# A layer with linear attention and a LoRA feed-forward: the shared expert's down factors are multiplied into the down weights on chip

## What is computed

```python
gate = x @ W_gate + lora(x, sA_gate, sB_gate) + expert_lora(x, A_gate, B_gate, w)
up = x @ W_up + lora(x, sA_up, sB_up) + expert_lora(x, A_up, B_up, w)
hidden = silu(gate) * up
out = hidden @ W_down + lora(hidden, sA_down, sB_down) + expert_lora(hidden, A_down, B_down, w)
```

## Time and profile before

| | before |
|---|---|
| median of 3 runs | 721.21 us (720.41 to 721.88) |
| the profiled execution: its own time | 720.7 us |
| the profiled execution: its span | 718.9 us |
| PE busy | 701.2 us (98%) |
| DVE busy | 376.2 us (52%) |
| ACT busy | 260.7 us (36%) |
| POOL busy | 122.3 us (17%) |
| read from HBM, written | 51.56 MB, 20.97 MB |

### The profile page before, as it was taken

One profiled execution on the slowest core, in us unless ns is written; L12 is line 12 of the kernel. 1 busy time (PEld: TensorE's weight loads), 2 busy tenths in 40 slices (PEclk: granted clock), 3 DMA queues, 4 the chain that ended last, 5 costly groups with the idle time before them and its releaser, 6 DMA issues.

```text
span 718.9 us, 10792 instructions
## 1 busy us (share of the span) xinstructions
PE 701.2 (98%) x3690; PEld 563.2 (78%) x3690; DVE 376.2 (52%) x715; ACT 260.7 (36%) x402; POOL 122.3 (17%) x293
## 2 busy tenths in 40 slices
PE   7999999989999999999999999999999999999997
PEld 5788888876776677888888888888888888888886
DVE  5666556677575675444427444336534435544434
ACT  4344334564331432333333333324333224323322
POOL 3554555420642651000000000000000000000000
PEclk9999999999999999999999999999999999999999
DMA  7756656326746635000010500001600001300001
GB/s 241 270 194 195 202 192 210 125 111 251 274 142 236 221 131 217 18 0 0 0 49 37 208 0 0 0 4 54 233 0 0 0 0 58 117 0 0 0 0 60
DMA packets 22755, 72.79 MB, mean 101 GB/s; under 512 B 2688, under 2 KB 2944, under 8 KB 20688
## 3 DMA queue, kind: packets, MB, share of 16 engines
q1 hardware_dynamic: 22560, 72.24, 28.4%
q0 software_dynamic: 176, 0.30, 0.2%
HBM read 51.56 MB, written 20.97 MB: 101 GB/s over the span
## 4 chain that ended last, share of the span: by engine, by line
PE 90%; DVE 4%; issue 2%; POOL 2%; ACT 1%; DMA 1%; SPq 0%; DVEq 0%; POOLq 0%; ACTq 0%
PE bank L1115 19%; PE bank L1116 19%; PE bank L1117 19%; PE bank L1328 17%; PE bank L1303 6%; PE bank L1315 4%; PE bank L1228 2%; DMA w_raw<-in_wkT 1%; PE bank L1180 1%; PE bank L1132 1%; PE bank L1152 1%; PE bank L1144 1%; PE bank L1236 1%; PE bank L1344 0%; PE bank L1346 0%
## 5 line engine op out<-in xcount | busy, mean ns | idle before, releaser
L1115 PE MATMUL bank<-x,up_h 128*128 (+1 forms) x352 | 137.5, 391 | 2.1 <-DVE qf L980 1.2
L1116 PE MATMUL bank<-x,up_h 128*128 (+1 forms) x352 | 137.3, 390 | 0.0
L1117 PE MATMUL bank<-x,up_l 128*128 (+1 forms) x352 | 137.0, 389 | 0.0
L1048 DVE TENSOR_TENSOR hf<-bank,silu 128x512 f32<-128x512 f32 x44 | 30.4, 692 | 162.3 <-issue 142.6
L1115 PEld LDWEIGHTS bank<-x,up_h 128*128 128x128 f32 x352 | 66.1, 188 | 18.8 <-issue 2.1
L597 ACT ACTIVATE hid_h<-hf 128x512 fp32r<-128x512 f32 x44 | 27.8, 632 | 142.9 <-DVE hf L1048 142.9
L1117 PEld LDWEIGHTS bank<-x,up_l 128*128 128x128 f32 x352 | 66.1, 188 | 14.1
L1116 PEld LDWEIGHTS bank<-x,up_h 128*128 128x128 f32 x352 | 66.1, 188 | 13.8
L793 DVE TENSOR_TENSOR up_l<-up_raw,up_h 128x1024 fp32r<-128x1024 f32 x45 | 55.6, 1235 | 31.4 <-ACT up_h L597 31.4
L1328 PE MATMUL bank<-dn_h,hid_h 128*128 128x512 f32 x176 | 69.5, 395 | 0.0
L1328 PE MATMUL bank<-dn_l,hid_h 128*128 128x512 f32 x176 | 69.1, 392 | 0.0
(11 more groups left out here) (167 smaller groups left out, 1228.3 us busy)
## 6 DMA issues: line engine op xcount, KB each, us to landing
x<-scr_x SPq DMA_DIRECT2D x8, 2048.0 KB, 7.5
up_raw<-in_ffn_up SPq DMA_DIRECT2D x11, 768.0 KB, 5.5
scr_x<-xt SPq DMA_DIRECT2D x16, 512.0 KB, 4.4
xin<-in_x SPq DMA_DIRECT2D x16, 256.0 KB, 5.8
scr_z<-zt SPq DMA_DIRECT2D x16, 256.0 KB, 2.2
x3r<-in_x SPq DMA_DIRECT2D x16, 256.0 KB, 3.5
scr_att<-x3r SPq DMA_DIRECT2D x16, 256.0 KB, 2.1
z<-scr_z SPq DMA_DIRECT2D x4, 1024.0 KB, 5.0
```

What stands on the lines that cost most here:

```text
L1048: nc.vector.tensor_tensor(hf[:], ps_u[:], silu[:], ALU.mult).then_inc(h_done, 1)
L1115: nc.tensor.matmul(dst, lh, rh, start=start, stop=False, **kw)
L1116: nc.tensor.matmul(dst, lh, rl, start=False, stop=False, **kw)
L1117: return nc.tensor.matmul(dst, ll, rh, start=False, stop=stop, **kw)
```

## The change

`W_down + sA_down @ sB_down / 8` is formed on chip and replaces W_down; the shared expert's columns leave the down operand, which shrinks from 592 to 576 columns. The product is made in stage 3: after `queries(g, (1, 2, 3))` of groups 1, 2 and 3, PE does one float32 matmul for each of 4, 4 and 3 chunks (`shared_down`), with 32 rows of contraction (8 of them not zero) at four different row positions of the array in turn, 128 output rows by 512 columns, into banks 2, 3, 4 and 5. DVE adds each bank, times 1/8, to the chunk in `dn_raw` in place, after its `queries` and ahead of its `attention(g - 1, (0, 1))`. PE's `denominators(g)`, which writes bank 2, now also waits for these additions (`dnm_done`), and ACT's first split of down weights waits for all 11. All down weights have to be there by then: SP loads them in stage 1, two chunks where it loaded one, and the two new constants (192 and 256 KB) ahead of wo and wq. PE's loop over groups 1 and 2 is unrolled.

`lora_down` takes two matmuls a chunk for three: the first has 128 stationary columns, the experts' 64 high and 64 low columns side by side, with the high part of the hidden values moving; the second has the 64 high columns with the low part moving. For that the split down weights lie in one tile `dn` of 9 blocks of 64 columns, high and low parts of a block next to each other, so the 512 columns that line 1328 reads are eight pieces of 64 with gaps of 64. Rows 64 to 127 of ps_zd then hold the low part's share; they are weighted like the others (`weights_of` copies twice, and two memsets at the start of the late stage go), zd1 takes all 128 rows, and `lora_down_lo` is one subtraction in place of two. ACT's extra rounding of 8 rows of `bdn` in stage 2 goes, and `bdn_done`, for which POOL and SP wait, comes from DVE.

```diff
@@ -46,2 +46,4 @@
-DNR = ER + 2 * R
-DNC = D + DNR
+DNC = D + ER
+DNB = DNC // ER
+SHG = P // DK
+SHN = -(-FC // SHG)
@@ -53 +55 @@
-STAGE2_LOADS = 8
+STAGE2_LOADS = 10
@@ -60 +62 @@
-    "ffn_up": (P, FC, UPC), "ffn_dn": (P, FC, DNC), "b_dn": (P, 2, D),
+    "ffn_up": (P, FC, UPC), "ffn_dn": (P, FC, DNC), "b_dn": (P, 2, D), "sa_dn": (P, SHN, P), "sb_dn": (P, D),
@@ -78,0 +81,2 @@
+        sa_dn = sb("sa_dn_sb", [P, SHN, P])
+        sb_dn = sb("sb_dn_sb", [P, D])
@@ -198,2 +202,2 @@
-        dn_h = at("dn_h", [P, 2, DNC], F32R)
-        dn_l = at("dn_l", [P, 2, DNC], F32R)
+        dn = at("dn", [P, 2, DNB, 2, ER], F32R)
+        dn_h, dn_l = dn[:, :, :, 0], dn[:, :, :, 1]
@@ -219,0 +224 @@
+        ps_sh = bank[2:6]
...
@@ -287,0 +291,2 @@
+        sh_ready = sem("sh_ready")
+        dnm_done = sem("dnm_done")
@@ -397 +402 @@
-            for dst, name in ((hmask, "headmask"), (hcol, "headcol"), (hrow_raw, "headrow"), (bdn_raw, "b_dn")):
+            for dst, name in ((hmask, "headmask"), (hcol, "headcol"), (hrow_raw, "headrow"), (bdn_raw, "b_dn"), (sa_dn, "sa_dn"), (sb_dn, "sb_dn")):
@@ -405,2 +410 @@
-            def load_ffn(c):
-
+            def load_up(c):
@@ -407,0 +412,2 @@
+
+            def load_dn(c):
@@ -414 +420,2 @@
-                load_ffn(p)
+                load_up(p)
+                load_dn(2 * p)
@@ -417 +424,4 @@
-            load_ffn(TILES // 2 - 3)
+                load_dn(2 * p + 1)
+            load_up(TILES // 2 - 3)
+            for c in range(TILES - 6, FC):
+                load_dn(c)
...
@@ -718,2 +727,0 @@
-            act.wait_ge(bdnl_done, 1)
-            round_to(bdn[SH:SH + R, 1], bdn_raw[SH:SH + R, 1]).then_inc(bdn_done, 1)
@@ -737 +745 @@
-                round_to(dn_h[:, s, :], dn_raw[:, bass.ds(c, 1), :].rearrange("p o n -> p (o n)")).then_inc(dnh_done, 1)
+                round_to(dn_h[:, s], dn_raw[:, bass.ds(c, 1), :].rearrange("p o (b n) -> p (o b) n", n=ER)).then_inc(dnh_done, 1)
@@ -761,2 +769,2 @@
-                round_to(zd1[0:ER, :], zw[0:ER, :])
-                round_to(zd2[0:DNR, :], zw[0:DNR, :]).then_inc(zdh_done, 1)
+                round_to(zd1[:], zw[:])
+                round_to(zd2[0:ER, :], zw[0:ER, :]).then_inc(zdh_done, 1)
@@ -778 +786 @@
-            act.wait_ge(dn_in, 16 * FC)
+            act.wait_ge(dnm_done, FC)
@@ -958,0 +967,8 @@
+            def shared_down(g, n=SHG):
+
+                for i in range(n):
+                    c = (g - 1) * SHG + i
+                    dve.wait_ge(sh_ready, c + 1)
+                    w = dn_raw[:, bass.ds(c, 1), 0:D].rearrange("p o n -> p (o n)")
+                    nc.vector.scalar_tensor_tensor(w, ps_sh[i][:], RSCALE, w, ALU.mult, ALU.add).then_inc(dnm_done, 1)
+
@@ -961,0 +978 @@
+                    shared_down(g, FC - (GROUPS - 2) * SHG if then is not None else SHG)
@@ -1010 +1027 @@
-            sub(bdn[0:SH2, 1], bdn_raw[0:SH2, 1], bdn[0:SH2, 1]).then_inc(bdnl_done, 1)
+            sub(bdn[0:ER, 1], bdn_raw[0:ER, 1], bdn[0:ER, 1]).then_inc(bdn_done, 1)
@@ -1033 +1050 @@
-                sub(dn_l[:, s, :], dn_raw[:, bass.ds(c, 1), :].rearrange("p o n -> p (o n)"), dn_h[:, s, :]
+                sub(dn_l[:, s], dn_raw[:, bass.ds(c, 1), :].rearrange("p o (b n) -> p (o b) n", n=ER), dn_h[:, s]
@@ -1056,3 +1073,4 @@
-                nc.vector.tensor_copy(wcur[:, :, 0:ER].rearrange("p j (e r) -> p j e r", e=E),
-                                      wtok[:, bass.ds(g * GT, GT), :].unsqueeze(3).to_broadcast([P, GT, E, R])
-                                      ).then_inc(wcur_done, 1)
+                for a in range(2):
+                    last = nc.vector.tensor_copy(wcur[:, :, a * ER:(a + 1) * ER].rearrange("p j (e r) -> p j e r", e=E),
+                                                 wtok[:, bass.ds(g * GT, GT), :].unsqueeze(3).to_broadcast([P, GT, E, R]))
+                last.then_inc(wcur_done, 1)
@@ -1063 +1081 @@
-                nc.vector.tensor_tensor(zw[0:DNR, :], ps_zd[0:DNR, :], wexp[0:DNR, :], ALU.mult).then_inc(zw_done, 1)
+                nc.vector.tensor_tensor(zw[:], ps_zd[:], wexp[:], ALU.mult).then_inc(zw_done, 1)
@@ -1067,2 +1085 @@
-                sub(zd1[ER:2 * ER, :], zw[0:ER, :], zd1[0:ER, :])
-                sub(zd2[SH2:SH2 + R, :], zw[SH:SH + R, :], zd2[SH:SH + R, :]).then_inc(zdl_done, 1)
+                sub(zd2[ER:2 * ER, :], zw[0:ER, :], zd2[0:ER, :]).then_inc(zdl_done, 1)
@@ -1085,3 +1101,0 @@
-                    nc.vector.memset(wcur[:, :, ER:], RSCALE)
-                    nc.vector.memset(zd2[:].bitcast(F32), 0.0).then_inc(late_clear, 1)
-                    dve.wait_ge(late_clear, 1)
@@ -1225,0 +1240 @@
+                wait(pe, dnm_done, min(g * SHG, FC))
@@ -1270,0 +1286,11 @@
+            def shared_down(g):
+
+                cs = range((g - 1) * SHG, min(g * SHG, FC))
+                pe.wait_ge(s2_in, 16 * STAGE2_LOADS)
+                pe.wait_ge(dn_in, 16 * (cs[-1] + 1))
+                pe.wait_ge(qn_done, g * KD)
+                for c in cs:
+                    strip = slice(c % SHG * DK, (c % SHG + 1) * DK)
+                    nc.tensor.matmul(ps_sh[c % SHG][:], sa_dn[strip, c // SHG, :], sb_dn[strip, :],
+                                     start=True, stop=True).then_inc(sh_ready, 1)
+
@@ -1273,0 +1300 @@
+                shared_down(g)
@@ -1282 +1309 @@
-            with pe.Fori(1, GROUPS - 1) as g:
+            for g in range(1, GROUPS - 1):
@@ -1314,4 +1341,4 @@
-                    for i, (h, w) in enumerate(((hid_h, dn_h), (hid_h, dn_l), (hid_l, dn_h))):
-                        d = nc.tensor.matmul(ps_zd[0:DNR, :], w[:, s, D:], h[:, s, :], start=(first and i == 0),
-                                             stop=(last and i == 2), skip_group_check=True)
-                    return d
+                    nc.tensor.matmul(ps_zd[:], dn[:, s, DNB - 1].rearrange("p a n -> p (a n)"), hid_h[:, s, :], start=first,
+                                     stop=False, skip_group_check=True)
+                    return nc.tensor.matmul(ps_zd[0:ER, :], dn_h[:, s, DNB - 1], hid_l[:, s, :], start=False, stop=last,
+                                            skip_group_check=True)
@@ -1328 +1355 @@
-                        d = nc.tensor.matmul(ps_out[j][:], h[:, s, cols], w[:, s, 0:D], start=(first and i == 0), stop=False,
+                        d = nc.tensor.matmul(ps_out[j][:], h[:, s, cols], w[:, s, 0:DNB - 1], start=(first and i == 0), stop=False,
@@ -1422 +1449 @@
-    ffn_dn = np.concatenate([given["W_down"], experts_in(given["A_down"]), given["sA_down"], given["sA_down"]], axis=1)
+    ffn_dn = np.concatenate([given["W_down"], experts_in(given["A_down"])], axis=1)
@@ -1424,0 +1452,6 @@
+    sa_dn, sb_dn = np.zeros((P, SHN, P), f32), np.zeros((P, D), f32)
+    for c in range(FC):
+        rows = given["sA_down"][c * P:(c + 1) * P]
+        sa_dn[c % SHG * DK:c % SHG * DK + R, c // SHG, :rows.shape[0]] = rows.T
+    for i in range(SHG):
+        sb_dn[i * DK:i * DK + R] = given["sB_down"]
...
```

More of the change, by code:

```diff
@@ L230, in program @@
         dene_done = sem("dene_done")
-        late_clear = sem("late_clear")
         wseth_done = sem("wseth_done")
@@ L285, in program @@
         bdnh_done = sem("bdnh_done")
-        bdnl_done = sem("bdnl_done")
         zd_ready = sem("zd_ready")
+        sh_ready = sem("sh_ready")
+        dnm_done = sem("dnm_done")
         x3_in = sem("x3_in")
@@ L459, in _ @@
             for c in range(early, FC - GROUPS + 2):
-                load_ffn(c)
+                load_up(c)
             with sp.Fori(0, GROUPS - 2) as g:
@@ L463, in _ @@
                 x3_load(g + 2)
-                load_ffn(g + FC - GROUPS + 2)
+                load_up(g + FC - GROUPS + 2)
                 att_store(g, True)
@@ L1438 @@
         "ffn_up": ffn_up, "ffn_dn": chunked(padded(ffn_dn, wide, DNC)),
-        "b_dn": blocks(experts_out(given["B_down"]), given["sB_down"]),
+        "b_dn": np.tile(experts_out(given["B_down"])[None], (2, 1, 1)).reshape(P, 1, D).repeat(2, axis=1),
+        "sa_dn": sa_dn, "sb_dn": sb_dn,
         "ident": np.eye(P, dtype=f32), "headmask": np.repeat(np.eye(HC, dtype=f32), DK, axis=0),
```

## The result

| | before, measured beside it | after |
|---|---|---|
| median of 5 runs | 721.88 us (720.41 to 723.07) | 714.34 us (713.89 to 716.27) |
| ratio, with its 95% interval | | 0.9895 (0.9874 to 0.9917) |
| the profiled execution: its own time, its span | 720.7, 718.9 us | 714.12, 712.3 us |
| its mean TensorE clock | 1.000 | 0.998 |

The kernel is 1.05% faster. The forecast was 714.8 us in a range of 713.6 to 718.3, so the number came out. Its working did so only in part: a gain and a loss that it did not contain nearly cancelled.

The account below looks back on a forecast made before the run. PE, busy 98% of the span, was taken to bound the kernel. 720.7 - 10.0 (LoRA products) + 3.8 (new float32 products) = 714.5 us, forecast as a median of 714.8 us after anchoring; range 713.6 to 718.3.

Parts of the forecast that it names:

- One product a chunk, 10.0 us: Late stage on PE: dropping one of three LoRA matmuls in each of 44 chunks saves 0.228 us each, 10.0 us.
- The twelve products stay at 2.75 to 2.78 us: Late stage on PE: the twelve down-projection products of each chunk keep their time, 2.75 to 2.78 us.
- The rival built on this layout: Line 1328, late stage: reading 64-column pieces with gaps lengthens each slot, by a tenth giving 726.6 us; chance 0.06.
- The strips, 3.8 us: Stage 3 on PE: 11 float32 products at different row positions overlap, adding 1.3, 1.3 and 1.2 us, 3.8 in all.
- the 0.29 of the denominators: Stage 3 on PE: time lost at the edges of eight float32 denominator passes, 0.29 us, reused to price the new products.
- Two at a time: Stage 3 strips: only one product's second pass overlaps the next one's first; 6.9 us added, 717.6 us total; chance 0.25.
- One after another: Stage 3 strips: no overlap between row positions, 10.3 us added, 721.0 us total, no change; chance 0.1.
- the extra time for each increment of a semaphore: Stage 3 strips: 26.3 ns per increment by the skill's rule, making the sum 0.2 us larger; mentioned on the side.
- DVE, nothing: Stage 3: 11 additions of 0.69 us on DVE add nothing to the path, with 1.0 us to spare before the denominators.
- Loads and constants in stage 1, nothing: Stage 1: earlier down loads and two new constants cost nothing, at worst 1 us.
- The tail, nothing: End of the last group: one 0.69 us subtraction goes, but PE's fillers set the first `lora_add`, so no gain counted.
- The anchor: Whole kernel: the sum starts from the profiled 720.7 us, 0.5 us under the median; the forecast lies midway between both anchors.

Follow-up runs that it names:

- the variant in one piece: Changed kernel with the high and the low 512 down-weight columns each lying contiguous, only the two LoRA blocks side by side; ratio 0.9879.
- the single row position: Changed kernel with all shared products at the array's first 32 rows instead of four row positions; 725.46 us, ratio 1.0036.
- the doubled ones: Changed kernel with each of DVE's 11 additions done as two additions of half the product; 717.86 us, ratio 0.9928.
- the padded kernel before: Kernel before with dn_h and dn_l in rows of 640 columns instead of 592, still three LoRA products a chunk; one run, 720.44 us.

## Why the prediction was right, and where it was not

**One product a chunk, 10.0 us.** Right in mechanism and near in size. Outside the twelve products a chunk went from 9.81 - 2.765 = 7.045 us to 9.54 - 2.72 = 6.82: 0.225, times 44 is 9.9. Alone, in the kernel before, it was worth 9.3; the 0.6 between the two are not explained.

**The twelve products stay at 2.75 to 2.78 us.** Wrong, and this is the step that failed. The prediction asked only whether the new layout could make them slower. It read 0.232 a product for one piece and 0.2275 for pieces, took this as proof that pieces do no harm, and did not ask why one piece was the slower. The chain said that 2.78 (the one in the earlier trace rows) and 2.75 alternate, which no difference in work explains. The place of the rows in memory does: 44 x 0.045 = 2.0 us in the twelve products, a gain that the sum left out. The rival built on this layout is out: eight pieces cost as much as one (the variant in one piece), and the slots moved the other way.

**The strips, 3.8 us.** Measured 3.7 between the landmarks of the two traces, 3.9 by leaving them out. The estimate took the middle between three at a time and wholly side by side. The equal times of six and eight passes, and the starts 7 ns apart, show that they are wholly side by side, and that the edges are larger than the 0.29 of the denominators: 1.26 - 0.86 = 0.4 us. Two errors of 0.1 us cancel. "Two at a time" (0.25) would have been 2.4 and 2.0 us. It falls, and the reason is in the order of the passes: the rival put the two passes of a product next to each other, and the trace has the first passes of all four products ahead of all second ones. So what falls is the conclusion that the rival drew, that a second strip cannot start before the first one's second pass. The rule of the Trainium skill that stood beside it ("TensorE: Matmul & The Clock Gate", "The mechanism"), that matmuls start and end in program order, is neither borne out nor refuted: in what order the four products stand among themselves cannot be read from the trace. "One after another" (0.1) is what the single row position shows: from slot to slot 194.63 - 190.35 less two slots of 0.23, 3.82 us for the 3.73 that were worked out, again with edges of 0.4. Of the extra time for each increment of a semaphore that the Trainium skill gives ("TensorE: Matmul & The Clock Gate", "The cost: per-tile semaphore tail") nothing is to be seen on PE's path: four increments and three differ by 0.01 us. PE's next product does not wait for these increments, so the tail itself is not measured.

**DVE, nothing.** Right. The margin was 1.5 us for the 1.0 forecast: the additions follow one another every 0.62 us, not 0.69, and the doubled ones show the point at which they begin to cost.

**Loads and constants in stage 1, nothing.** Not refuted. Stage 1 is 0.6 us longer in the trace of after, but half of it is there before any new load is issued: the first weights land at 8.07 us for 7.77. The other half lies in POOL's wait from about 13 to 20 us, and that took 7.12 us in the padded kernel before, which has no new constant, and 6.38 in the changed kernel with doubled additions, which has. It varies from run to run.

**The tail, nothing.** The prediction held that PE's fillers set the time of the first `lora_add`, and counted nothing for the subtraction that goes. By the timeline of after that was not the whole of it:

```profile
704.98 1.50 PE L1194 MATMUL bank<-ident_sb 128*128 128x128 f32 x12
706.29 0.50 PE L1371 MATMUL bank<-bdn,zd 128*128 128x512 f32 x1
```

The first `lora_add` now comes 1.31 us behind the first filler, where it came 712.61 - 711.13 = 1.48 us behind it; before, the second subtraction ended at 711.17 + 1.38 = 712.55, 0.06 ahead of it, so DVE set the time. That is 0.17 of the 0.45 us; the rest lies behind the last additions on DVE, and no run here was made for it.

**The anchor.** The profiled execution of before was not a typical one. In 37 executions of it beside the experiments, four have a clock of 1.000, and spans of 718.2 to 719.2 us; 33 have 0.994 to 0.998, and 719.9 to 722.9. The sum started from one of the four and is compared with a median of the others. Of the 33, 23 have 0.994 or 0.995, which in the profiled executions goes with two falls, one of them in stage 1. The changed kernel falls too: its profiled execution lost 1.4 us in stage 2 to the clock, and not to the change. This and the start of stage 1, +2.0 together, stood against the 2.0 of the twelve products and 0.45 at the tail: that is why 714.8 fitted, and it was luck. One execution of the changed kernel had a clock of 0.999 and a span of 710.0 us. Against the spans of before at full clock, 718.2 to 719.2, the change is worth 8.2 to 9.2 us, where the sum had 10.0 - 3.8 = 6.2; the parts that belong to the change add up to 9.9 - 3.7 + 2.0 + 0.45 = 8.65.

## What to carry to other kernels

Price a removed instruction by its slot in the chain, and small independent float32 products by their overlap at different row positions; both held here to 0.2 us, though the second with two errors of 0.1 us in a product's price that cancelled. When equal work takes two alternating times in a trace, follow it up: padding rows to a multiple of 512 bytes shortened each product of the down projection here by some 4 ns, and the trace of before hinted at it. Look at the granted clock of several executions before anchoring on one profile.

## What the runs showed of the hardware

- A float32r product of 512 columns took 0.231 us instead of 0.227 when its moving operand started 64 bytes off a multiple of 512, counted from the start of the tile (2.77 against 2.72 us for twelve), and 0.234 when it started 128 bytes off. With 256 bytes off it took 0.227.
- Three or four float32 products of 32 rows at different row positions took 1.07 us of the chain; the same four at one position took 3.62. The first passes of all of them started within 0.02 us, and the second passes 0.53 us later. In the type float32r four took 0.44.
- Behind products on 32 rows, without a pause, the clock fell to 1.2 GHz for some 3.5 us in groups 1 (3.6 us of such products) and 3 (2.8), and not in group 2 (3.6). Between 150 and 156 us, behind pauses of 0.6 and 1.2 us, it fell in seven of the eleven profiled executions without fillers and in none of the three with them. What decides between the seven and the four stays open. Five of all fourteen have a fall at 10 to 15 or 28 to 33 us.
